# Offset products of the up weights: weights as the moving side in four column tiles, result rows turned into columns through DRAM

## The reference

```
h = (h - mu) / sqrt(var + 1e-05) * lg + lb        # lg, lb: 256 values a layer
h = h @ w1 + b1                                   # w1: 256 x 1364
a, g = split(h, 2, axis=-1)
h = a * gelu(g)
x = x + h @ w2 + b2
```

## Time and profile before

| | us |
|---|---|
| time, median of 3 runs (772.13 to 774.22) | 772.15 |
| time of the profiled execution | 772.45 |
| its span, from first to last instruction | 770.7 |
| PE busy in the span | 718.7 (93%) |
| DVE / ACT / POOL busy | 498.9 / 494.3 / 462.6 |

### The profile page before, as it was taken

One profiled execution on the slowest core, in us unless ns is written; L12 is line 12 of the kernel. 1 busy time (PEld: TensorE's weight loads), 2 busy tenths in 40 slices (PEclk: granted clock), 3 DMA queues, 4 the chain that ended last, 5 costly groups with the idle time before them and its releaser, 6 DMA issues.

```text
span 770.7 us, 16909 instructions
## 1 busy us (share of the span) xinstructions
PE 718.7 (93%) x4952; PEld 595.8 (77%) x4952; DVE 498.9 (65%) x1424; ACT 494.3 (64%) x1321; POOL 462.6 (60%) x646
## 2 busy tenths in 40 slices
PE   5989899899999999999999998999999999999957
PEld 4878787587878787878787867788787878787847
DVE  1376772785858585858585858666676767676732
ACT  3656634566666767676758686858585857575742
POOL 1467662695747474747575767757474747474722
PEclk9999995899999999999999999999999999999998
DMA  5664460150000000000000001010101010101000
GB/s 146 227 208 131 113 217 0 56 188 15 28 16 27 14 27 14 27 14 27 14 28 15 28 2 55 2 55 0 54 0 54 0 54 0 54 0 41 1 29 14
DMA packets 32795, 38.46 MB, mean 50 GB/s; under 512 B 8476, under 2 KB 22896, under 8 KB 32752
## 3 DMA queue, kind: packets, MB, share of 16 engines
q1 hardware_dynamic: 32752, 37.95, 15.5%
HBM read 29.55 MB, written 8.39 MB: 49 GB/s over the span
## 4 chain that ended last, share of the span: by engine, by line
PE 64%; issue 10%; DVE 9%; POOL 7%; ACT 7%; DMA 1%; ACTq 0%; DVEq 0%; POOLq 0%; SPq 0%
PE ps L448 35%; PE ps L655 5%; PE ps L614 4%; PE ps L641 3%; POOL pr L1494 3%; PE ps L632 2%; ACT pr L928 2%; PE ps L548 2%; PE ps L626 2%; PE ps L659 2%; PE ps L643 1%; PE ps L642 1%; PE ps L441 1%; DVE hT_lo L1189 1%; DVE arena L1052 1%
## 5 line engine op out<-in xcount | busy, mean ns | idle before, releaser
L1494 POOL TENSOR_SCALAR pr<-pr,rl 128x128 f32<-128x128 f32 (+1 forms) x256 | 108.7, 438 | 89.8 <-DVE rl L1222 89.5
L928 ACT ACTIVATE pr<-sm,mn 128x128 f32<-128x128 f32 (+1 forms) x256 | 113.5, 447 | 9.7 <-DVE mn L1216 9.0
L448 PE MATMUL ps<-hT_hi,w_hi 128*128 128x256 f32 (+1 forms) x352 | 105.3, 299 | 3.6 <-DVE hT_lo L1189 1.4
L1216 DVE CUSTOM_DVE_ANT_0 sm<-ps,wmask 128x128 f32<-128x128 f32 (+1 forms) x256 | 80.1, 354 | 33.8 <-PE ps L632 29.9
L448 PE MATMUL ps<-hT_hi,w_lo 128*128 128x256 f32 (+1 forms) x352 | 99.6, 283 | 0.0
L448 PE MATMUL ps<-hT_lo,w_hi 128*128 128x256 f32 (+1 forms) x352 | 99.2, 282 | 0.0
L888 ACT ACTIVATE sqb<-ps 128x512 f32<-128x512 f32 x64 | 38.0, 596 | 92.8 <-PE ps L448 90.3
L1464 POOL TENSOR_TENSOR rn<-ss,nhalf 128x16 f32<-128x16 f32 x32 | 95.2, 2975 | 2.7
L448 PE MATMUL ps<-wqkv_hi,yT_hi 128*128 128x512 f32 x192 | 78.8, 411 | 1.6 <-DVE arena L1073 1.6
L448 PE MATMUL ps<-wqkv_lo,yT_hi 128*128 128x512 f32 x192 | 75.9, 395 | 0.0
L448 PE MATMUL ps<-wqkv_hi,yT_lo 128*128 128x512 f32 x192 | 75.9, 395 | 0.0
(11 more groups left out here) (169 smaller groups left out, 2137.3 us busy)
## 6 DMA issues: line engine op xcount, KB each, us to landing
arena<-x SPq DMA_DIRECT2D x16, 256.0 KB, 3.0
ystream<-arena SPq DMA_DIRECT2D x16, 256.0 KB, 2.1
y_next<-ystream SPq DMA_DIRECT2D x16, 256.0 KB, 2.8
y_res<-ystream SPq DMA_DIRECT2D x16, 256.0 KB, 2.7
arena<-L_ffn_w SPq DMA_DIRECT2D x5, 640.0 KB, 4.7
arena<-ctx SPq DMA_DIRECT2D x8, 256.0 KB, 4.2
arena<-mask_BxSxS_ik SPq DMA_DIRECT2D x8, 256.0 KB, 3.4
xmid<-arena SPq DMA_DIRECT2D x8, 256.0 KB, 2.1
```

What stands on the lines that cost most here:

```text
L448: last = mm(out, lhsT(a), rhs(b), start=(start and i == 0), stop=(stop and i == 2))
L928: A(pr[:, h % NS, a:b], sm[:, h % NS, a:b], ACT.Exp, bias=mn[:, h, t:t + 1], scale=-1.0, accum_out=ls[:, h, t:t + 1]).then_inc(e_done, 1)
L1216: V.tensor_tensor_reduce(sm[:, h % NS, a:b], bank(h % SB)[:, a:b], wmask[:, a:b], 1.0, -NEG, ALU.add, ALU.min, mn[:, h, t:t + 1]).then_inc ...
L1494: G.tensor_scalar(pr[:, h % NS, a:b], pr[:, h % NS, a:b], rl[:, h, t:t + 1], 1.0, ALU.mult, ALU.mult).then_inc(pn_done, 1)
```

## The change

`bias_products` is turned round. The single column `lgb[:, l, 1, k:k+1]` is now the stationary side (128 rows, one column), and w1 is the moving side: its 1386 columns in SBUF are cut into four runs of 347, 347, 347 and 345 columns. Run i writes one row at PSUM partition 32*i, so the four runs stand in four column tiles of the array. That is 2 x 4 products a layer, 16 records where there were 44.

The result is a row, and a bias must be a column. ACT's new `offsets_out(l)` copies 128 x 347 of PSUM to SBUF (into `gl` and `u_pair`, which are free in step 0), SP's new `turn_offsets(l)` stores the four rows to DRAM, waits until they are stored, and loads them as columns into `offset_col` with four DMAs of single elements. `fold_offset` reads `offset_col`; it now stands after `low_oT(PAIRS - 2)`, behind the softmax of step 0, and waits for all eight column loads (`col_in`). PE's `weighted` of step 0 waits for `row_out`, for bank 5 and 6 to be free.

```diff
@@ block.sync
+            def turn_offsets(l):
+                sp.wait_ge(row_out, l + 1)
+                for i in range(4):
+                    sp.dma_start(offsets[l, i * RP:(i + 1) * RP].unsqueeze(0),
+                                 offset_row[l][32 * i:32 * i + 1, 0:RP]).then_inc(row_stored, 16)
+                sp.wait_ge(row_stored, 64 * (l + 1))
+                for half in range(2):
+                    sp.dma_start(offset_col[:, l, half, 0:HC - 1],
+                                 offsets[l, half * HF:(half + 1) * HF].rearrange("(c p) -> p c", p=P),
+                                 allow_slow_non_contiguous=True).then_inc(col_in, 16)
+                    o = 2 * HF + half * GT
+                    sp.dma_start(offset_col[half * GT:half * GT + HT, l, half, HC - 1:HC],
+                                 offsets[l, o:o + HT].unsqueeze(1),
+                                 allow_slow_non_contiguous=True).then_inc(col_in, 16)
...
@@ step(s, la, lf) of block.sync
                 if isinstance(s, int) and s == 0:
+                    for l in range(DEPTH):
+                        turn_offsets(l)
                     store_mid(NB - 2)
                     load_residual(NB - 1)
@@ block.tensor
                 w1_in = raws(l)[2]
-                for c in range(HC):
-                    for o, r, n in up_parts(c):
-                        for k in range(KC):
-                            last = mm(ps[0:r, b1_bank[l], n * HC + c:n * HC + c + 1],
-                                      w1_in[:, k, o:o + r], lgb[:, l, 1, k:k + 1],
-                                      start=(k == 0), stop=(k == KC - 1))
+                for k in range(KC):
+                    for i, (o, n) in enumerate(row_parts):
+                        last = mm(ps[32 * i:32 * i + 1, b1_bank[l], 0:n], lgb[:, l, 1, k:k + 1],
+                                  w1_in[:, k, o:o + n], start=(k == 0), stop=(k == KC - 1))
                 last.then_inc(b1_mm, 1)
...
                     elif lf is not None:
                         pe.wait_ge(u_done, HC * s)
+                    else:
+                        pe.wait_ge(row_out, pair + 1)
@@ block.scalar
+                def offsets_out(l):
+                    act.wait_ge(b1_mm, l + 1)
+                    A(offset_row[l][:, 0:RP], bank(b1_bank[l])[:, 0:RP], ACT.Copy).then_inc(row_out, 1)
...
@@ block.vector
-                dve.wait_ge(b1_mm, l + 1)
-                sums = ps[:, b1_bank[l], 0:2 * HC].rearrange("p (h c) -> p h c", h=2)
-                V.tensor_tensor(b1_sb[:, l, :, 0:HC - 1], b1_sb[:, l, :, 0:HC - 1], sums[:, :, 0:HC - 1],
+                dve.wait_ge(col_in, 64 * DEPTH)
+                V.tensor_tensor(b1_sb[:, l, :, 0:HC - 1], b1_sb[:, l, :, 0:HC - 1], offset_col[:, l, :, 0:HC - 1],
                                 ALU.add).then_inc(b1_done, 1)
...
@@ step 0 of block.vector
                 if start:
                     dve.wait_ge(cst2_in, CONSTS)
-                    fold_offset(0)
-                    fold_offset(1)
...
                     low_oT(PAIRS - 2)
+                    if start:
+                        fold_offset(0)
+                        fold_offset(1)
```

More of the change, by code:

```diff
@@ L72, in build @@
     xmid = nc.dram_tensor("xmid", [NB, P, T * D], F32, kind="Internal").ap()
+    offsets = nc.dram_tensor("offsets", [DEPTH, 4 * ((W1C + 3) // 4)], F32, kind="Internal").ap()
     ystream = nc.dram_tensor("ystream", [STEPS, P, T * D], F32, kind="Internal").ap()
@@ L162, in build @@
         u = [sb(f"u_{n}", [P, HC, S], F32R) for n in ("hi", "lo")]
+        offset_row = [t[:].rearrange("p a n -> p (a n)") for t in (gl, u_pair)]
+        offset_col = sb("offset_col", [P, DEPTH, 2, HC])
         assert W1C <= 3 * T * D and HC * D <= 4 * 3 * P
@@ L180, in build @@
         w2_copied = sem("w2_copied")
+        row_out, row_stored, col_in = sem("row_out"), sem("row_stored"), sem("col_in")
         b1_mm, b1_done, w1_scaled = sem("b1_mm"), sem("b1_done"), sem("w1_scaled")
@@ L234, in build @@
         b1_bank = (5, 6)
+        RP = (W1C + 3) // 4
+        row_parts = [(i * RP, min(RP, W1C - i * RP)) for i in range(4)]
         def raws(l):
@@ L968, in step @@
                     values(1)
+                if isinstance(s, int) and s == 0:
+                    offsets_out(0)
                 if lf is not None:
@@ L978, in step @@
                     keys_T(0)
+                if isinstance(s, int) and s == 0:
+                    offsets_out(1)
                 if lf is not None:
@@ L1110, in fold_offset @@
                     b = b1_sb[q:q + HT, l, half, HC - 1:HC]
-                    V.tensor_tensor(b, b, sums[q:q + HT, 0, HC - 1:HC], ALU.add).then_inc(b1_done, 1)
+                    V.tensor_tensor(b, b, offset_col[q:q + HT, l, half, HC - 1:HC], ALU.add).then_inc(b1_done, 1)
             def low_yT(n):
```

## The result

| | before | after |
|---|---|---|
| time, median (us) | 772.14 | 766.05 (765.42 to 766.87, 4 runs) |
| ratio | 1 | 0.9916 [0.9902, 0.9931] |
| profiled execution / its span (us) | 772.45 / 770.7 | 766.11 / 764.3 |
| PE busy (us) | 718.7 | 707.8 |

The change makes the kernel faster by 0.84%, 6.1 us by the medians. The forecast of 764.0 is 2.05 us too low; the range 760.0 to 768.5 holds the time.

What follows compares the result with a forecast made beforehand. Step 0's stage was taken as bound by PE, 18.2 us alone, 14.57 of it offset products. A gain of 8.4 less 0.2 for the fold gave 8.2 us, so 772.15 to about 764.0, range 760.0 to 768.5.

Steps and rivals of the forecast that it cites:

- Their cost is in columns streamed: New offset products, step 0: 0.845 ns a column at full clock, so 0.293 us per 347-column record, 0.586 at half.
- four at once: New offset products: four column tiles overlap fully, 1.17 us a layer at full clock, 2.35 at half.
- Rival 1: Offset products' tiles run in a row or two at a time; 765.3 to 770.9 us; chance 0.13.
- I take it as fallen: PE's clock at layer 1's products, from 115.2 us: half clock, so they take 2.35 us, to 117.55.
- DVE's second scaling ends at 116.57 and is just covered: Step 0, before the last transposes: the scaling they need ends before layer 1's products do at 117.55 us.
- The fold: Six small DVE instructions moved ahead of step 0's last oT_lo: 0.85 us, of which 0.2 us not covered.
- The turn: Offset rows stored to DRAM and loaded as columns: landed by 136.6 us at the latest, before the fold at 140.4.
- rival 3: Turn through DRAM is late, so the fold waits and holds DVE's last oT_lo; 765 to 772 us; chance 0.04.
- What the clock takes back: Step 0 after the shift: low clock over the part now at 1.00 costs up to 2.8 us, giving 766.8.
- Rival 2: PE's clock stays high or comes back early in step 0; 759.5 to 762 us; chance 0.14.
- Rival 4: Layer 1's products: a column-tile record costs more than a whole-array one and none overlaps; slower, 780 us; chance 0.03.
- two tiles run fully side by side: Weighted values' 64-column tiles, step 1: 4 records of 128 columns take 0.22 us, against 0.43 one after another.

Runs made afterwards that it cites:

- one_tile: Changed kernel with all four runs of w1 columns written to one PSUM partition, so one column tile; 765.97 us, ratio 0.9906.
- wide_before: Kernel before, old orientation and 44 records a layer, with 128 columns of the shift matrix moving instead of one; 765.43 us, ratio 0.9898.
- pool_later: Changed kernel with POOL's scaling of w1 held until DVE's second scaling is done; 764.31 us, ratio 0.9890.
- fold_early: Changed kernel with both folds back at their old place, ahead of the first row minima; 767.77 us, ratio 0.9924.
- no_turn: Changed kernel without the stores and loads through DRAM and without the folds, products and evacuations kept; 766.32 us, ratio 0.9904.
- after_again: The changed kernel run once more, unaltered, with its own profile; 766.76 us, ratio 0.9907.
- keep_busy_pool_later: Changed kernel with thrown-away 512-column products in PE's step 0 gaps and POOL's w1 scaling held until DVE's second scaling; 762.59 us, ratio 0.9859.
- wide_true_pool_later: Kernel before with lb's column broadcast to 128 moving columns, blocks reordered, POOL's w1 scaling held until DVE's second scaling; 768.02 us, ratio 0.9931.

## Why the prediction came out as it did

- **The stage is bound by PE, and the products are the cost: right.** But the price was put on the wrong thing. "Their cost is in columns streamed" and "four at once" were right as sizes for the wide records (1.17 us a layer forecast, groups 0.29 us apart measured, 1.34 from the first start to the last end, and none of the loss that 2.38 for three tiles, in the Trainium skill, "TensorE: Matmul & The Clock Gate", section "Measured speedup vs the span model", would give), and they do not decide. one_tile and wide_before have the gain without them. Of the 8.1 us won before the first exponential, 6.6 are there with 44 records of 128 columns at the full clock (21.48 - 14.84); only some 1.4 us come from the short products, and at the last oT_lo 0.6 of them are left (32.34 against 32.97), which the time can't tell. Rival 1 had this case: tiles in a row with the clock held high, 765.3; one_tile is 765.97.
- **"I take it as fallen": wrong, but not for every execution.** When layer 1's products start, the clock is still at 1.00, and they take 1.34 us with their tail, not 2.35. Seven of the profiled executions have these products on PE in four tiles and nothing put in beside them. In five of them the clock fell 7.0 to 7.3 us after the first product, behind layer 1's products; in pool_later and fold_early it fell after 5.0 and 4.4 us, ahead of them, and they took 2.49 us. Fold_early shows that it would have made no difference to the chain: its last transposes waited for DVE even so, and started 8.25 us after the first product.
- **"DVE's second scaling ends at 116.57 and is just covered": wrong.** The duration was taken from the earlier trace rows, where DVE begins 0.3 us ahead of POOL. In the changed kernel POOL need not wait for the products any more and begins 0.74 us ahead of DVE, and the same instruction takes 2.33 us. What was missed is a consequence that the prediction itself named: POOL starts "1.14 us earlier" was booked as cover, not as a collision. The runs show it both ways (1.22 to 1.23 with POOL held back, in four profiles; 2.33 to 2.34 without, in nine). The Trainium skill, "SBUF — State Buffer", section "Who interferes with whom", says that a VectorE instruction with two inputs in SBUF contends with a GpSimd one that reads SBUF, and that issue order decides who blocks. This case agrees in direction: DVE loses nothing when it is first (1.22), and 1.11 us when POOL is. POOL loses in either order: its two instructions take 1.44 and 1.43 us alone, 2.23 and 1.42 when DVE is first, 2.01 and 2.38 when POOL is. So here being first does not keep an instruction from being slowed; whether either engine is blocked outright for part of the time, the trace can't tell.
- **These two errors cancel, which is luck.** Forecast was 115.2 + 2.35 = 117.55 for the start of the transposes, 8.11 us after the first product; measured 8.33. Behind that lie products that started 5.18 us after the first one (5.76 forecast, so w1 came 0.6 us sooner) and were through at 6.5, and then a wait for DVE. The transposes took 1.94 us against 1.82. So the gain at that point was 8.1 where 8.4 was forecast: right in size for the wrong reasons.
- **The fold: 0.2 us charged, 0 measured**, with 0.29 us of idle time left. **The turn: hidden, as forecast** (no_turn); rival 3 is refuted, at the late place.
- **What the clock takes back: 0.5 us**, inside the bounds given (up to 2.8). The prediction named a longer stretch from the first exponentials to the last oT_lo as a sign of being wrong, "then the clock or the fold took the gain back". By this sign it was wrong by a little: 18.95 us (18.72 in after_again) where it was 18.49. It was not the fold. The low clock covers 11.0 us of that stretch, and 9.7 before, and over the 14 profiled executions the stretch is by and large the longer, the more of it is at the low clock: 17.81 us with 3.4 at the low clock, 18.05 to 18.19 with 6.8, 18.16 to 18.49 with 8.8 to 9.7, 18.69 to 19.35 with 10.2 to 11.6.
- **The rest of the miss is not the change.** Of the 1.86 us between the forecast for the profiled execution (764.25) and its time (766.11), 8.2 - 7.63 = 0.57 arise in step 0 (0.3 ahead of the first exponential, 0.5 behind it, less the 0.2 for the fold) and 1.33 ahead of it, in a part that no edit touches (last section); -0.10 behind it and 0.06 outside the span make up the rest. That the prediction took the one execution's start as every execution's was its other weakness: the median of before was itself 772.14 to 774.22 in four sets of runs, so the ratio, not the time, is the thing to forecast.
- Rival 2 (clock high: 759.5 to 762) did not come by itself, but it is what keep_busy_pool_later was built to bring about: 762.59 with 774.22 beside it. Rival 4 is refuted by the 4.76 us of 16 records in one tile, 0.298 us each where 0.293 was forecast, and by the groups of four that start together.
- One reading stood on less than it said: "two tiles run fully side by side" rests on the 0.22 us of the earlier trace rows and on the earlier trace rows, while the 0.58 us of the four wider records in the earlier trace rows is more than the 0.43 that two full tiles would give. Four tiles then did run side by side.

What stays open: what brings on the low-clock stretch in the cross-attention part, why the clock falls earlier in some executions than in others with the same work on PE, and how much pool_later alone is worth in time.

## What to carry to other kernels

A PE that is busy at 100% with one-column products is not a PE at work: before a layout is turned round, look at the granted clock under it, and try a wide moving side (a broadcast is enough) at the same place. When a chain on one engine is cut short, take every engine that it released and ask what that engine's earlier work now overlaps: an instruction's duration from the trace holds only for the neighbours that it had there. And where a store and a load stand in the way of a value, move its use, not the transfer.

## What the runs showed of the hardware that was not expected

- The clock's fall. In the kernel before it fell to 0.50 at 113.3, under the first 44-record string of one-column products and with PE busy without a gap. It stayed at 1.00 in the window of 13 us in which PE was busy all the time, mostly with 347 columns in one tile (one_tile), over the 11.7 us of products and transposes of 128 columns (wide_before), and also from 109 to 118 in the changed kernel, where PE was busy for 2.51 of the last 6 us. There it fell only afterwards, at 118.1.
- In some executions there is a low stretch in the cross-attention part, before anything that was changed. The window 19 to 23 us, before and after:

```profile
19.00:23.00 4.00, 3.81 (x19) 3.24 (x20) 0.93 (x6) 1.77 (x5) 0.00 (x0) 1.00 0.73 238
```

```profile
19.00:23.00 4.00, 4.00 (x13) 3.11 (x12) 0.00 (x0) 1.53 (x5) 0.00 (x0) 0.57 0.79 262
```

  It goes with the start of the first product in all 14 profiled executions: the six that have such a stretch of 3.4 us (at 19 or at 57 to 58 us: after, one_tile, pool_later, wide_true_pool_later, no_turn, fold_early) start it at 110.72 to 111.27, the eight without (before among them) at 109.13 to 109.72. Which kernel it is plays no part that could be seen.
- Small stores beside a large load: 3.4 us from the last issue to the notice beside w1's 1.4 MB, 0.9 us without it. That the load is the reason is not shown.
- The low stretch near the end of the kernel was 10.2 us long after (739.3 to 749.5) and 6.8 before (748.2 to 755.0), and yet the time from the last oT_lo of step 0 to the end was the same, 621.2 and 621.3 us.
